# Expert lists padded to 128 rows instead of 256 in the mixture-of-experts stage of a four-stage kernel

## The chip, the core and the metric

The program runs on one core of a Trainium2 chip. The metric is device time in microseconds (us) for one execution; a comparison is made between medians of executions on the same chip. The core has five engines that run their own instruction streams and meet through semaphores: PE (TensorE, matrix products), DVE (VectorE), ACT (ScalarE), POOL (GpSimd) and SP (SyncE, which issues DMAs here). Times in a trace are us from the span's start unless marked ns.

## The reference, cut to what matters

Four layers run one after the other on an input of 2 x 2048 tokens of 128 features. The last one, cut from the reference, is the one that the change touches:

```python
x = hidden_states.reshape(T, D)                       # 4096 tokens of 128
logits = x @ gate_w + gate_b                          # 8 experts
probs = jax.nn.softmax(logits.astype(jnp.float32), axis=-1)
top_w, top_idx = jax.lax.top_k(probs, TOP_K)          # TOP_K = 2
top_w = top_w / jnp.sum(top_w, axis=-1, keepdims=True)
combine = jnp.zeros((T, NUM_EXPERTS), jnp.float32)
combine = combine.at[jnp.arange(T)[:, None], top_idx].set(top_w)
h = jax.nn.silu(jnp.einsum('td,edf->tef', x, w1)) * jnp.einsum('td,edf->tef', x, w3)   # f = 512
out_e = jnp.einsum('tef,efd->ted', h, w2)
out = jnp.einsum('ted,te->td', out_e, combine)
...
x = x + _layernorm(_L1_ffn_ref(_layernorm(x, axis=-1), ...), axis=-1)
```

The kernel computes only the two chosen experts of each token: 4096 tokens x 2 = 8192 pairs of a token and an expert.

## The kernel before, in words

The last stage is `phase_moe`. Its order is written out by hand in one list for each engine.

**Lists.** DVE finds the two experts of each token, counts the pairs of each expert and gives every pair a place: the pairs of an expert stand together, and each expert's list is padded to a whole number of tiles of ROWS = 256 rows. TILES = 39 tiles hold any split of 8192 pairs over 8 experts. `grid` and `tiles_of` count the tiles of an expert, `place` and `pos` the pair's place, `past` and `expert` the expert of each tile. The lists are turned by products with one-hot matrices (`hot_soon` for the first 16 columns of 128 rows, `hot_late` for the other COLS - 16 = 62) into `source`, the row that each place reads, and `to`, the row that it writes.

**Tile loop.** A tile of 256 rows goes through these steps:

- POOL issues two indirect DMAs that gather 128 rows each into `g` (`gather`, L2277), six tiles ahead (AHEAD = 6) into eight buffers.
- PE loads the tile's expert number from the list `expert` into a register (`expert_of`, L2133), and turns the rows by four products with the identity (`x_turn`, L2093); DVE copies them into `x16` (L2507).
- A tile has two units (u = 0, 1) of 256 hidden features. `up` makes a unit: for each of two blocks of 128 features, and for w1 (`R1`) and w3 (`R3`), one `product` of three matmuls in float16 parts (L2014 to L2016), with 256 columns. The weights' address depends on the expert's register (`of_expert`).
- ACT takes silu (L2231), DVE multiplies (L2523), ACT and DVE split the result into two float16 parts (L2217, L2514).
- `down` makes the second layer of a unit three units later (LAG = 3): twelve matmuls of 128 columns (L2126 to L2128), for two blocks of features and two halves r of 128 rows.
- ACT copies a finished tile to `y` (L2223), and POOL issues two indirect DMAs that scatter it to `moe_outs` (L2296).

PE's own order is

```python
for n in range(UNITS):
    i, u = divmod(n, 2)
    up(n, es[i])
    if u == 0 and i + 1 < TILES:
        es[i + 1] = expert_of(i + 1)
        x_turn(i + 1)
    if n >= LAG:
        down(n - LAG, es[(n - LAG) // 2])
```

and POOL's is, for each tile i: scatter tile i (two DMAs), then gather tile i + 6 (two DMAs).

**After the loop** SP reads `moe_outs` back, and DVE, ACT, POOL and PE add each token's two rows, normalise and add to `X`.

Of the kernel before, what the change touches and what calls it, by code (L numbers as in the profile page):

```python
# [8 lines left out]
ALU = mybir.AluOpType  # L9
# [3 lines left out]
P = 128  # L13
B = 2
T = 2048
# [9 lines left out]
E = 8  # L25
# [25 lines left out]
def build(nc, xT, vecs, att_w, cv_w, tern_w, hid_w, w3_w, ssm_w, dt_w, moe_w13, moe_w2, gate_w, consts, selectors, iota_c, outT,  # L51
# [3 lines left out]
    with ctx:  # L55
# [80 lines left out]
        if last_phase >= 4:  # L136
            phase_moe(nc, G)
        else:
            finish(nc, ctx, X, outT)
# [1717 lines left out]
def phase_moe(nc, G):  # L1857
# [6 lines left out]
    CHUNKS = GROUPS * TC  # L1864
    PAIRS = 2 * CHUNKS
    ROWS = 2 * P
    TILES = (PAIRS * P + E * (ROWS - 1)) // ROWS
    COLS = 2 * TILES
    UNITS = 2 * TILES
    PARTS = 8  # L1870
    PP = PAIRS // PARTS
    QUARTERS = 4
    QP = PAIRS // QUARTERS
    GRID = B * T // ROWS
    AHEAD, GR, HR, YR = 6, 8, 4, 4

    SOON, LATE = 16, COLS - 16
# [2 lines left out]
    with mem:  # L1880
        def sb(name, shape, dt=F32):
            return mem.enter_context(nc.sbuf_tensor(name, shape, dt))

        I32, U32 = mybir.dt.int32, mybir.dt.uint32
# [4 lines left out]
        lane_f = sb("lane_f4", [P, P])  # L1889
# [26 lines left out]
        so_far = sb("so_far4", [P, E, CHUNKS], F16)  # L1916
        grid = sb("grid4", [P, E, GRID])
        tiles_of = sb("tiles_of4", [P, E])
        tiles_to = sb("tiles_to4", [P, E])
# [6 lines left out]
        col_i = sb("col_i4", [P, PAIRS], I32)  # L1926
        col_h = sb("col_h4", [P, PAIRS], F16)
        low_h = sb("low_h4", [P, PAIRS], F16)
        past = sb("past4", [1, TILES, E])
        expert_f = sb("expert_f4", [1, TILES])  # L1930
        expert = sb("expert4", [1, TILES], I32)
        row_f = sb("row_f4", [P, COLS])
        empty = sb("empty4", [P, COLS])
        second = sb("second4", [P, COLS])
# [7 lines left out]
        x16 = sb("x16_4", [P, 2, 2, ROWS], F16)  # L1942
# [5 lines left out]
        w13_hi, w13_lo = G.moe_hi[:, 0:E, :], G.moe_lo[:, 0:E, :]  # L1948
        w2_hi, w2_lo = (w[:, E:, :].rearrange("p u m -> p (u m)").rearrange("p (e m) -> p e m", e=E)
                        for w in (G.moe_hi, G.moe_lo))  # L1950
# [18 lines left out]
        rank = XG[:, 1, 0:E * CHUNKS].rearrange("p (e c) -> p e c", e=E)  # L1969
# [24 lines left out]
        def _(sp):  # L1994
# [5 lines left out]
            for r in range(YR):  # L2000
                sp.wait_ge(S[f"scattered{r}"], 32 * len(range(r, TILES, YR)))
            by_pair = outs[0:P * PAIRS, :].rearrange("(p k c) d -> p k c d", k=2, c=CHUNKS)
# [9 lines left out]
        def _(pe):  # L2012
            def product(out, w_hi, w_lo, x_hi, x_lo, start, stop):
                nc.tensor.matmul(out, w_hi, x_hi, start=start, stop=False)  # L2014
                nc.tensor.matmul(out, w_hi, x_lo, start=False, stop=False)  # L2015
                return nc.tensor.matmul(out, w_lo, x_hi, start=False, stop=stop)  # L2016
# [54 lines left out]
            for q in range(PARTS):  # L2071
# [3 lines left out]
                for k in range(q * PP, (q + 1) * PP):  # L2075
                    last = nc.tensor.matmul(listed_soon, low_hot[:, k, :], hot_soon[:, k, 1:3, :].rearrange("p w c -> p (w c)"),
                                            start=k == 0, stop=k == PAIRS - 1)
            last.then_inc(S["listed"], 1)
            for q in range(QUARTERS):
                pe.wait_ge(S["hot_part"], q + 2)  # L2080
                pe.wait_ge(S["hot_pair"], q + 2)
                for k in range(q * QP, (q + 1) * QP):
                    last = nc.tensor.matmul(listed_late, low_hot[:, k, :], hot_late[:, k, 1:3, :].rearrange("p w c -> p (w c)"),  # L2083
                                            start=k == 0, stop=k == PAIRS - 1)
# [12 lines left out]
            def of_expert(w, e, m):  # L2097
                return w[:, bass.ds(e, 1), m].rearrange("p a m -> p (a m)")

            def up(n, e):
                i, u = divmod(n, 2)
                if u == 0:
                    pe.wait_ge(S["x_in"], i + 1)
                if n >= 2:
                    pe.wait_ge(S["hidden"], n - 1)
                for h in range(2):
                    for out, at in ((R1, 0), (R3, FFN)):
                        m = slice(at + (2 * u + h) * P, at + (2 * u + h + 1) * P)
                        last = product(out[:, u, h * ROWS:(h + 1) * ROWS], of_expert(w13_hi, e, m), of_expert(w13_lo, e, m),  # L2110
                                       x16[:, i % 2, 0, :], x16[:, i % 2, 1, :], True, True)
                last.then_inc(S["up"], 1)

            def down(n, e):
                i, u = divmod(n, 2)
                pe.wait_ge(S["hid_low"], n + 1)
                if u == 0 and i >= 2:
                    pe.wait_ge(S["y_out"], i - 1)
                for h in range(2):  # L2120
                    m = slice((2 * u + h) * P, (2 * u + h + 1) * P)
                    w_hi, w_lo = of_expert(w2_hi, e, m), of_expert(w2_lo, e, m)
                    for r in range(2):
                        out = Y[:, i % 2, r * P:(r + 1) * P]
                        at = slice(h * ROWS + r * P, h * ROWS + (r + 1) * P)
                        nc.tensor.matmul(out, hid_hi[:, n % HR, at], w_hi, start=u == 0 and h == 0 and r == 0, stop=False)  # L2126
                        nc.tensor.matmul(out, hid_hi[:, n % HR, at], w_lo, start=False, stop=False)  # L2127
                        last = nc.tensor.matmul(out, hid_lo[:, n % HR, at], w_hi,  # L2128
                                                start=False, stop=u == 1 and h == 1 and r == 1)
                last.then_inc(S["down"], 1)  # L2130

            def expert_of(i):
                return pe.value_load(expert[0:1, i:i + 1], min_val=0, max_val=E - 1)  # L2133

            pe.wait_ge(S["expert"], 1)
            es = {0: expert_of(0)}
            x_turn(0)
# [8 lines that stand above are left out]
            for n in range(UNITS - LAG, UNITS):  # L2146
                down(n, es[n // 2])

            for i in range(GROUPS):
# [3 lines left out]
                for j in range(TC):  # L2153
                    last = nc.tensor.matmul(R1[:, i % 2, j * P:(j + 1) * P], scaled[:, i % 2, j * P:(j + 1) * P], G.ident,
                                            start=True, stop=True)
# [159 lines left out]
        def _(dve):  # L2315
# [42 lines left out]
            def last_expert(v):  # L2358
# [18 lines left out]
                                           op0=ALU.mult, op1=ALU.add).then_inc(S["masked"], 1)  # L2377
# [21 lines left out]

            dve.wait_ge(S["counted"], 1)  # L2400
            steps = lane_f[:, 0:GRID].unsqueeze(1).to_broadcast([P, E, GRID])
            nc.vector.scalar_tensor_tensor(out=grid[:, :, :], in0=steps, scalar=float(ROWS),
                                           in1=counts.unsqueeze(2).to_broadcast([P, E, GRID]),
                                           op0=ALU.mult, op1=ALU.is_lt).then_inc(S["grid"], 1)
            dve.wait_ge(S["grid"], 1)
# [7 lines left out]
            dve.wait_ge(S["tiles_from"], 1)  # L2413
            dve.wait_ge(S["ranked"], 1)
            nc.vector.scalar_tensor_tensor(out=place[:, :, :], in0=tiles_from[:, :].unsqueeze(2).to_broadcast([P, E, CHUNKS]),
                                           scalar=float(ROWS), in1=rank, op0=ALU.mult, op1=ALU.add)\
              .then_inc(S["place"], 1)
            dve.wait_ge(S["place"], 1)
            nc.vector.tensor_tensor(placed[:, :, :, :], picks[:, :, :, :],
# [14 lines left out]
                                           op0=ALU.mult, op1=ALU.add).then_inc(S["low_h"], 1)  # L2434
# [39 lines left out]
            def targets(listed, c, n):  # L2474
                by_part = listed[:, 0:c.stop - c.start]
                nc.vector.scalar_tensor_tensor(out=empty[:, c], in0=by_part, scalar=0.0, in1=spare_f[:, c],
                                               op0=ALU.is_equal, op1=ALU.mult).then_inc(S["empty"], 1)
                nc.vector.scalar_tensor_tensor(out=row_f[:, c], in0=by_part, scalar=float(PAIRS), in1=row_f[:, c],
                                               op0=ALU.mult, op1=ALU.add).then_inc(S["row_f"], 1)
                dve.wait_ge(S["empty"], n + 1)  # L2480
                dve.wait_ge(S["row_f"], 2 * n + 2)
                nc.vector.scalar_tensor_tensor(out=to[:, c], in0=row_f[:, c], scalar=-float(PAIRS), in1=empty[:, c],
                                               op0=ALU.add, op1=ALU.add).then_inc(S["to"], 1)

            sources(listed_soon, slice(0, SOON), 0)
            for q in range(1, QUARTERS):
# [1 line left out]
                pair(hot_late, slice((q - 1) * QP, q * QP), LATE, q + 1)  # L2488
            pair(hot_late, slice((QUARTERS - 1) * QP, PAIRS), LATE, QUARTERS + 1)
            targets(listed_soon, slice(0, SOON), 0)  # L2490
            nc.vector.tensor_tensor(past[:, :, :], tiles_to[0:1, :].unsqueeze(1).to_broadcast([1, TILES, E]),
                                    lane_f[0:1, 0:TILES].unsqueeze(2).to_broadcast([1, TILES, E]), ALU.is_le)\
              .then_inc(S["past"], 1)
            dve.wait_ge(S["past"], 1)
            nc.vector.tensor_reduce(expert_f[:, :], past[:, :, :], AX.X, ALU.add).then_inc(S["expert_f"], 1)
# [22 lines left out]
            for n in range(UNITS):  # L2518
                i, u = divmod(n, 2)
                dve.wait_ge(S["silus"], n + 1)  # L2520
                if n >= HR:
                    dve.wait_ge(S["hid_low"], n - HR + 1)
                nc.vector.scalar_tensor_tensor(out=hid[:, n % HR, :], in0=R3[:, u, :], scalar=1.0 / WS,  # L2523
                                               in1=silu[:, u, :], op0=ALU.mult, op1=ALU.mult).then_inc(S["hidden"], 1)
# [105 lines left out]
```

## Time and profile before

| | |
|---|---|
| median of 3 executions | 1307.19 us (1306.41 to 1311.79) |
| the profiled execution, its own time | 1311.32 us |
| its span | 1309.6 us |
| mean granted clock of PE | 0.923 of 2.4 GHz |
| busy, share of the span | PE 82%, DVE 75%, ACT 56%, POOL 56% |
| tile loop: first register instruction of `up` to the last | 1065.2 to 1263.0 us |

The profiled execution is one of the program's executions with the hardware profiler on; its own time is 4.1 us above the median, and 1.7 us of it lie outside the span. A busy share is an average over the four stages, which have different limits; the tile loop is about 15% of the span, so it is read by windows of time and by single instructions. Matmuls are pipelined: a PE row's duration reaches past the start of the next, and the pace of PE is the distance between starts.

### The profile page before, as it was taken

How to read it: one execution, taken by the hardware profiler on the slowest of the kernel's cores; microseconds unless marked ns; L12 is line 12 of the kernel's file. 1: busy time of each engine (PE TensorE's matmuls, PEld its weight loads, DVE VectorE, ACT ScalarE, POOL GpSimd, SP SyncE). 2: the span in 40 equal slices, each digit the busy share in tenths (PEclk: the TensorE clock that was granted, in tenths of full speed). 3: DMA queues.
4: the chain of work that ended last, by engine and by line, in shares of the span. 5: the costliest groups of instructions: out<-in, count | busy, mean ns of one | idle time of the engine just before them, and what ended most of it. 6: DMA issues, size and time to landing. Idle time of an engine off the chain costs nothing. (4 is left out here: it accounts for less than half of the span.)

```text
span 1309.6 us, 16592 instructions
## 1 busy us (share of the span) xinstructions
PE 1072.4 (82%) x4914; PEld 542.1 (41%) x4914; DVE 987.7 (75%) x1333; ACT 733.9 (56%) x1163; POOL 737.6 (56%) x617
## 2 busy tenths in 40 slices
PE   6654679999999988989889898989788578887863
PEld 2211224444444432333333333434234468776753
DVE  6996776575755537999999999999992776655545
ACT  6774454555645445757667676757653345444444
POOL 0223342141422103899898989897984157777764
PEclk8885799999999998999999999999999579999996
DMA  6000000000000002323223222222220111111225
GB/s 226 1 1 0 0 1 1 1 2 1 0 0 0 1 0 90 105 72 103 75 92 93 84 89 88 65 73 72 66 65 0 65 28 50 53 49 51 49 46 192
DMA packets 32552, 67.07 MB, mean 51 GB/s; under 512 B 5760, under 2 KB 5952, under 8 KB 32256
## 3 DMA queue, kind: packets, MB, share of 16 engines
q1 hardware_dynamic: 27056, 55.16, 12.9%
q0 software_dynamic: 4992, 10.23, 2.9%
q8 instruction: 39, 0.64, 0.2%
q10 hardware_dynamic: 432, 0.76, 0.2%
q14 instruction: 33, 0.27, 0.1%
HBM read 56.57 MB, written 9.57 MB: 51 GB/s over the span
## 5 line engine op out<-in xcount | busy, mean ns | idle before, releaser
L1750 POOL TENSOR_TENSOR prod<-hs,csb 128x1024 f32<-128x1024 f32 x128 | 301.8, 2358 | 142.3 <-DVE hs L1797 141.6
L1797 DVE TENSOR_TENSOR_SCAN hs<-dA,carry,pD 128x512 f32<-128x512 f32 x256 | 313.7, 1267 | 5.2 <-DVE pD L1810 0.8
L1519 PE MATMUL pY<-prod,const 128*128 128x512 f32 x512 | 244.8, 601 | 1.8 <-POOL prod L1750 1.8
L1659 ACT ACTIVATE dA<-dt,negA 128x512 f32<-128x512 f32 x256 | 168.0, 713 | 17.3 <-POOL dt L1719 15.8
L1810 DVE TENSOR_TENSOR pD<-dtu,pD 128x1024 f32<-128x1024 f32 x128 | 155.6, 1216 | 9.7 <-PE pD L1533 9.6
L1519 PEld LDWEIGHTS pY<-prod,const 128*128 128x128 f32 x512 | 96.8, 192 | 117.7 <-issue 112.9
L2277 POOL DMA_INDIRECT g<-moe_rows,source x78 | 82.8, 1061 | 57.3 <-DVE source L2472 27.9
L2523 DVE SCALAR_TENSOR_TENSOR hid<-pR,silu 128x512 f32<-128x512 f32 x78 | 53.9, 691 | 68.0 <-ACT silu L2231 67.9
L1003 ACT ACTIVATE stage<-pR,vec 128x512 f32<-128x512 f32 x64 | 43.9, 687 | 100.2 <-PE pR L703 100.0
L2296 POOL DMA_INDIRECT moe_outs<-y,to x78 | 81.6, 1046 | 26.9 <-issue 23.2
L2231 ACT ACTIVATE silu<-pR 128x512 f32<-128x512 f32 x78 | 46.6, 597 | 75.7 <-PE pR L2016 75.7
L2014 PE MATMUL pR<-x,moe_hi 128*128 128x256 f16 x312 | 85.7, 275 | 2.4 <-DVE x L2507 2.4
L2015 PE MATMUL pR<-x,moe_hi 128*128 128x256 f16 x312 | 85.6, 274 | 0.0
L2016 PE MATMUL pR<-x,moe_lo 128*128 128x256 f16 x312 | 85.6, 274 | 0.0
L1448 PE MATMUL pQ<-xn,convw 128*128 128x512 f32 x112 | 61.5, 675 | 16.9 <-DVE xn L1780 16.9
L1053 POOL TENSOR_TENSOR z_lo<-z,z_hi 128x512 f16<-128x512 f32 x8 | 10.6, 1329 | 106.1 <-DVE z_hi L1140 106.1
L439 POOL TENSOR_TENSOR o<-o,rs 128x512 f32<-128x512 f32 x8 | 14.4, 1799 | 96.8 <-DVE o L559 96.8
L1533 PE MATMUL pD<-split,sel 96*128 96x512 bf16 x128 | 50.5, 395 | 19.0 <-DVE hs L1797 18.3
L1042 POOL TENSOR_TENSOR K_lo<-kstage,K_hi 128x512 f16<-128x512 f32 x24 | 28.8, 1204 | 53.7 <-DVE K_hi L1115 53.7
L2126 PE MATMUL pY<-moe_hi,hid_hi 128*128 x312 | 56.7, 220 | 0.8 <-DVE hid_lo L2514 0.8
L2128 PE MATMUL pY<-moe_hi,hid_lo 128*128 x312 | 56.6, 220 | 0.0
L2127 PE MATMUL pY<-moe_lo,hid_hi 128*128 x312 | 56.6, 220 | 0.0
(423 smaller groups left out, 2573.9 us busy)
## 6 DMA issues: line engine op xcount, KB each, us to landing
csb<-ssm_c SPq DMA_DIRECT2D x128, 256.0 KB, 3.1
raw<-moe_w SPq DMA_DIRECT2D x12, 512.0 KB, 4.9
room<-moe_outs SPq DMA_DIRECT2D x8, 512.0 KB, 7.9
hidw<-hid_w SPq DMA_DIRECT2D x1, 2048.0 KB, 10.0
moe_rows<-xt SPq DMA_DIRECT2D x8, 256.0 KB, 2.0
outT<-X SPq DMA_DIRECT2D x8, 256.0 KB, 2.0
X<-xT SPq DMA_DIRECT2D x3, 512.0 KB, 4.1
g<-moe_rows,source POOLq DMA_INDIRECT x78, 2.8
```

The source lines that it names most:

```text
L1448: last = nc.tensor.matmul(Q[c][:], convw[:, c, k, :], xn[b][:, k:k + N], start=k == 0, stop=k == TAPS - 1)
L1519: last = nc.tensor.matmul(YB[c][:], G.ident, prod[:, slot(b, n), c, :], start=n == 0, stop=n == DST - 1)
L1659: last = nc.scalar.activation(dA[:, slot(b, n), c, :], dt[:, b, c, :], ACT.Exp, scale=negA[:, c, n:n + 1])
L1750: nc.gpsimd.tensor_tensor(prod[:, slot(b, n), :, :], hs[:, slot(b, n), :, :], csb[:, slot(b, n), :, :].to_broadcast([P, CB, N]), ALU.mult)\
L1797: last = nc.vector.tensor_tensor_scan(hs[:, slot(b, n), c, :], dA[:, slot(b, n), c, :], dBu(n, c), carry[:, b, n, c:c + 1], ALU.mult, ALU.add)
L1810: nc.vector.tensor_tensor(DD[:, (n % 2) * CB:(n % 2) * CB + CB, :], dtu[:, b, :, :], bcastB(n).unsqueeze(1).to_broadcast([P, CB, N]), ALU. ...
L2014: nc.tensor.matmul(out, w_hi, x_hi, start=start, stop=False)
L2015: nc.tensor.matmul(out, w_hi, x_lo, start=False, stop=False)
L2016: return nc.tensor.matmul(out, w_lo, x_hi, start=False, stop=stop)
L2126: nc.tensor.matmul(out, hid_hi[:, n % HR, at], w_hi, start=u == 0 and h == 0 and r == 0, stop=False)
L2277: nc.gpsimd.indirect_dma_start(g[:, i % GR, r, :], None, rows, bass.IndirectOffsetOnAxis(ap=source[:, 2 * i + r:2 * i + r + 1], axis=0))\
L2296: nc.gpsimd.indirect_dma_start(outs, bass.IndirectOffsetOnAxis(ap=to[:, 2 * i + r:2 * i + r + 1], axis=0), y[:, i % YR, r, :], None).then_ ...
```

## The change

The unit of padding becomes 128 rows. An expert's list is padded to a multiple of 128, TILES becomes 36, and a tile still has 256 rows, but its two halves r = 0, 1 may belong to two experts. So PE loads two expert numbers for each tile, and every product of `up` is made for each half apart, with 128 columns and the half's own weights. `down` takes its weights inside the loop over halves.

```diff
-    TILES = (PAIRS * P + E * (ROWS - 1)) // ROWS
+    TILES = ((PAIRS * P + E * (P - 1)) // P + 1) // 2
...
-    GRID = B * T // ROWS
+    GRID = B * T // P
...
-        past = sb("past4", [1, TILES, E])
-        expert_f = sb("expert_f4", [1, TILES])
-        expert = sb("expert4", [1, TILES], I32)
+        past = sb("past4", [1, COLS, E])
+        expert_f = sb("expert_f4", [1, COLS])
+        expert = sb("expert4", [1, COLS], I32)
...
                         m = slice(at + (2 * u + h) * P, at + (2 * u + h + 1) * P)
-                        last = product(out[:, u, h * ROWS:(h + 1) * ROWS], of_expert(w13_hi, e, m), of_expert(w13_lo, e, m),
-                                       x16[:, i % 2, 0, :], x16[:, i % 2, 1, :], True, True)
+                        for r in range(2):
+                            s = slice(r * P, (r + 1) * P)
+                            last = product(out[:, u, h * ROWS + r * P:h * ROWS + (r + 1) * P], of_expert(w13_hi, e[r], m),
+                                           of_expert(w13_lo, e[r], m), x16[:, i % 2, 0, s], x16[:, i % 2, 1, s], True, True)
...
-                    w_hi, w_lo = of_expert(w2_hi, e, m), of_expert(w2_lo, e, m)
                     for r in range(2):
+                        w_hi, w_lo = of_expert(w2_hi, e[r], m), of_expert(w2_lo, e[r], m)
...
-                return pe.value_load(expert[0:1, i:i + 1], min_val=0, max_val=E - 1)
+                return [pe.value_load(expert[0:1, c:c + 1], min_val=0, max_val=E - 1) for c in (2 * i, 2 * i + 1)]
...
-            nc.vector.scalar_tensor_tensor(out=grid[:, :, :], in0=steps, scalar=float(ROWS),
+            nc.vector.scalar_tensor_tensor(out=grid[:, :, :], in0=steps, scalar=float(P),
...
-                                           scalar=float(ROWS), in1=rank, op0=ALU.mult, op1=ALU.add)\
+                                           scalar=float(P), in1=rank, op0=ALU.mult, op1=ALU.add)\
...
-            nc.vector.tensor_tensor(past[:, :, :], tiles_to[0:1, :].unsqueeze(1).to_broadcast([1, TILES, E]),
-                                    lane_f[0:1, 0:TILES].unsqueeze(2).to_broadcast([1, TILES, E]), ALU.is_le)\
+            nc.vector.tensor_tensor(past[:, :, :], tiles_to[0:1, :].unsqueeze(1).to_broadcast([1, COLS, E]),
+                                    lane_f[0:1, 0:COLS].unsqueeze(2).to_broadcast([1, COLS, E]), ALU.is_le)\
```

COLS = 2 x TILES goes from 78 to 72, so `hot_late` from 62 columns to 56 and `past` from 312 numbers to 576; GRID goes from 16 to 32.

```order
L2014 ISA
L2014 MATMUL pR3_4<-x16_4,moe_hi 128x256
L2015 MATMUL pR3_4<-x16_4,moe_hi 128x256
L2016 REGISTER_ALU
L2016 MATMUL pR3_4<-x16_4,moe_lo 128x256
```

And now, for the same block of features:

```order
L2014 ISA
L2014 MATMUL pR3_4<-x16_4,moe_hi 128x128
L2015 MATMUL pR3_4<-x16_4,moe_hi 128x128
L2016 REGISTER_ALU
L2016 MATMUL pR3_4<-x16_4,moe_lo 128x128
L2014 ISA
L2014 MATMUL pR3_4<-x16_4,moe_hi 128x128
L2015 MATMUL pR3_4<-x16_4,moe_hi 128x128
L2016 REGISTER_ALU
L2016 MATMUL pR3_4<-x16_4,moe_lo 128x128
```

One pair of register instructions stood ahead of 768 columns, and now stands ahead of 384.

The second place is PE at the end of the first unit of a tile, where it loads the next tile's expert (expert4) and turns its rows (g4). Before:

```order
L2016 REGISTER_ALU
L2016 MATMUL pR3_4<-x16_4,moe_lo 128x256
L2133 TENSOR_LOAD expert4
L2133 ISA x2
L2093 MATMUL pX4<-ident16_4,g4 128x128 x4
```

And now:

```order
L2016 REGISTER_ALU
L2016 MATMUL pR3_4<-x16_4,moe_lo 128x128
L2135 TENSOR_LOAD expert4
L2135 ISA x2
L2135 TENSOR_LOAD expert4
L2135 ISA x2
L2093 MATMUL pX4<-ident16_4,g4 128x128 x4
```

A second load with its two followers stands between `up` and `x_turn`.

The third place is one block of features of `down` on PE (hid_hi4 and hid_lo4 are the parts of the hidden layer). Before:

```order
L2126 ISA
L2126 MATMUL pY4<-moe_hi,hid_hi4 128x128
L2127 REGISTER_ALU
L2127 MATMUL pY4<-moe_lo,hid_hi4 128x128
L2128 MATMUL pY4<-moe_hi,hid_lo4 128x128
L2126 MATMUL pY4<-moe_hi,hid_hi4 128x128
L2127 MATMUL pY4<-moe_lo,hid_hi4 128x128
L2128 MATMUL pY4<-moe_hi,hid_lo4 128x128
```

And now:

```order
L2128 ISA
L2128 MATMUL pY4<-moe_hi,hid_hi4 128x128
L2129 REGISTER_ALU
L2129 MATMUL pY4<-moe_lo,hid_hi4 128x128
L2130 MATMUL pY4<-moe_hi,hid_lo4 128x128
L2128 ISA
L2128 MATMUL pY4<-moe_hi,hid_hi4 128x128
L2129 REGISTER_ALU
L2129 MATMUL pY4<-moe_lo,hid_hi4 128x128
L2130 MATMUL pY4<-moe_hi,hid_lo4 128x128
```

The matmuls are the same six; the second half has a pair of register instructions of its own. Over the whole program PE had 312 pairs in `up` and 156 in `down` and now has 576 and 288; it had 39 loads of an expert number and now has 72. The waits of PE keep their places: one ahead of `x_turn` (L2090), one ahead of the first unit of a tile (L2106), one ahead of the first `down` of a tile (L2119, now L2121).

## Rows read from the trace of the kernel before

**Rows 1.** The page's part 4, the chain that ended last, by line.

```profile
POOL moe_outs L2296 4%; POOL g L2277 3%; DMA g<-moe_rows,source 1%; PE pX L2034 1%; DVE room L2451 1%; DMA room<-moe_outs 1%; DVE room L2438 0%; DVE hid L2538 0%; ACT convw L2245 0%; PE pR L2014 0%; PE pR L2016 0%; PE pR L2015 0%; PE pY L2083 0%; DVE room L2444 0%; PE pX L2026 0%
```

**Rows 2.** Groups of instructions from 980 us on: POOL's indirect DMAs (busy, mean ns | idle before).

```profile
L2277 POOL DMA_INDIRECT g<-moe_rows,source x78 | 82.8, 1061 | 57.3 <-DVE source L2472 27.9 <-issue 21.0 <-PE pR L2016 7.1
L2296 POOL DMA_INDIRECT moe_outs<-y,to x78 | 81.6, 1046 | 26.9 <-issue 23.2 <-ACT y L2223 3.7
```

**Rows 3.** Timeline of POOL: start, duration, engine, line, what [idle before].

```profile
1234.06 1.05 POOL L2296 DMA_INDIRECT moe_outs<-y,to  x1 [0.30 <-issue]
...
1239.52 1.05 POOL L2296 DMA_INDIRECT moe_outs<-y,to  x1 [0.30 <-issue]
```

**Rows 4.** Timeline of PE: down, up and the wait ahead of the next x_turn.

```profile
1155.70 0.22 PE L2126 MATMUL pY<-moe_hi,hid_hi 128*128 x1
...
1156.37 0.27 PE L2014 MATMUL pR<-x,moe_hi 128*128 128x256 f16 x1
...
1157.57 0.27 PE L2016 MATMUL pR<-x,moe_lo 128*128 128x256 f16 x1
1158.99 0.40 PE L2093 MATMUL pX<-ident,g 128*128 128x128 f16 x4 [1.15 <-DMA g<-moe_rows,source]
```

**Rows 5.** PE's expert loads from 1073 to 1095 us: ns min/median/max, first and last start.

```profile
L2133 PEldq TENSOR_LOAD <-expert x6: 297/302/308, 1073.3 to 1094.1; - x6
L2133 PEldq FUSED_REGOPS  x6: 151/151/151, 1073.7 to 1094.5; - x6
L2133 PEldq SEQ_ASSERT  x6: 18/18/18, 1073.9 to 1094.7; - x6
```

**Rows 6.** Lines L2014, L2016 and L2106 over the whole span, columns as in rows 5.

```profile
L2014 PEldq FUSED_REGOPS  x312: 46/46/51, 1065.2 to 1262.9; - x156
L2016 PEldq ALU_OP  x312: 32/32/38, 1065.3 to 1263.0; - x156
L2016 PE MATMUL pR<-x,moe_lo x312: 272/273/421, 1065.5 to 1264.4; 128*128 128x256 f16 x156
L2106 PEldq EVENT_SEMAPHORE  x38: 51/51/51, 1068.2 to 1260.5; - x38
```

**Rows 7.** Lines L2014 and L2126 from 1070.6 to 1072.0 us, and from 1074.0 to 1076.0 us.

```profile
L2014 PEldq FUSED_REGOPS  x4: 46/46/46, 1070.7 to 1071.4; - x4
...
L2126 PEldq FUSED_REGOPS  x2: 46/53/60, 1071.7 to 1071.9; - x2
...
L2126 PEldq FUSED_REGOPS  x4: 46/46/60, 1074.1 to 1075.9; - x4
...
L2014 PEldq FUSED_REGOPS  x4: 46/46/46, 1074.6 to 1075.4; - x4
```

**Rows 8.** Timeline of DVE while the lists are made.

```profile
1034.82 0.29 DVE L2402 SCALAR_TENSOR_TENSOR grid<-lane_f,pR 128x128 f32<-128x128 f32 x1 [0.29 <-PE pR L2067]
...
1050.40 1.18 DVE L2438 TENSOR_TENSOR room<-lane_h,col_h 128x992 f16<-128x992 f16 x1
...
1060.51 0.47 DVE L2491 TENSOR_TENSOR past<-tiles_to,lane_f 1x312 f32<-1x312 f32 x1
...
1062.70 0.22 DVE L2461 TENSOR_SCALAR second<-pY 128x62 f32<-128x62 f32 x1 [1.01 <-PE pY L2083]
```

**Rows 9.** Windows: length, busy of PE, PEld, DVE, ACT, POOL, granted clock, DMA share, GB/s.

```profile
1097.00:1204.00 107.00, 88.05 (x1059) 77.97 (x1060) 65.06 (x101) 52.12 (x101) 82.32 (x82) 1.00 0.18 51
1206.70:1210.10 3.40, 1.25 (x19) 0.96 (x17) 1.48 (x3) 1.11 (x2) 2.79 (x3) 1.00 0.21 65
1210.10:1213.50 3.40, 3.40 (x24) 2.65 (x22) 0.93 (x2) 0.79 (x2) 2.49 (x4) 0.50 0.19 33
```

**Rows 10.** Timeline of PE at the lower clock, an `up` and the `down` behind it.

```profile
1210.29 0.42 PE L2014 MATMUL pR<-x,moe_hi 128*128 128x256 f16 x1
...
1212.85 0.31 PE L2126 MATMUL pY<-moe_hi,hid_hi 128*128 x1
1212.95 0.31 PE L2127 MATMUL pY<-moe_lo,hid_hi 128*128 x1
```

## The prediction

> **What bounds the kernel now.** The change lies in the tile loop of the last stage, so I looked first at what sets the pace there. The chain that ended last [rows 1] holds three lines of this loop and names POOL's two, the scatter and the gather, ahead of PE's products; the other pieces are of other stages or of the ends of this one. The groups [rows 2] say why: 156 indirect DMAs, 1.05 us each, and after nearly each 0.3 us that the view calls issue. Busy 82.8 + 81.6 and idle 57.3 + 26.9, less the 27.9 us that POOL waited for the first list, make 220.7 us, 1.41 us for a call. A tile's four calls need 4 x (1.05 + 0.30) = 5.4 us, and in the timeline of POOL [rows 3] the first scatters of two tiles stand 5.46 us apart (1234.06 to 1239.52), with the 0.30 ahead of each: POOL is full.
>
> PE waits for it. In its timeline [rows 4] twelve matmuls of `down` take 1155.70 to 1156.37, 0.056 us each, each with weights of its own; the twelve of `up` with 256 columns go at 0.109 us (eleven steps, 1156.37 to 1157.57); and then the next `x_turn` waits 1.15 us for a gather. The array's work for a tile is 24 x 0.109 + 24 x 0.056 + 4 x 0.056 = 4.2 us, which is the pace early in the loop, while gathers were still ahead: expert loads recur every 4.16 us (1073.3 to 1094.1 in five tiles, [rows 5]). Over the whole loop, from the first register instruction of `up` at 1065.2 to the last at 1263.0 [rows 6], 39 tiles take 197.8 us, 5.1 us each.
>
> There is a third clock in this loop, which no busy time shows: PE's sequencer. Each product costs it two register instructions, FUSED_REGOPS of 46 ns and ALU_OP of 32 ns [rows 6]. Their durations are not their price. The price is read from starts where nothing held the sequencer [rows 7]: four FUSED_REGOPS of an `up` from 1070.7 to 1071.4 and two of the `down` behind it at 1071.7 and 1071.9 are six starts, five pairs in 1.2 us, 0.24 us a pair. The next such stretch goes from 1074.1 through the `up` at 1074.6 to 1075.4 to the `down` that ends at 1075.9: eight starts, seven pairs in 1.8 us, 0.257 us. A pair of `down` is followed by six matmuls and one of `up` by three, and both cost about a quarter of a microsecond: it is the register instructions that cost, not the matmuls. I take 0.245.
>
> An expert load takes the sequencer from 1073.3 (TENSOR_LOAD, 0.30 us) over FUSED_REGOPS (0.15) to SEQ_ASSERT at 1073.9 [rows 5], with what follows it about 0.65 us. A wait that is already met lasts 51 ns [rows 6]; a register instruction takes 0.24 / 2 = 0.12 us for durations near 0.04, some 0.08 more than it shows, so I estimate a wait at 0.11 to 0.13 and take 0.11. The sequencer's work for a tile before is then 12 x 0.245 + 0.65 + 3 x 0.11 = 3.9 us. So for each tile now: POOL 5.4, the array 4.2, the sequencer 3.9. It hides behind both.
>
> **The change, part by part.** *POOL* issues 144 calls in place of 156. At 1.41 us that is 17 us off the engine that bounds the loop; for a tile its work stays at 5.4 to 5.7 us.
>
> *The array* streams the same columns for a tile: 48 matmuls of 128 columns in `up`, for 24 of 256. If 128 columns take what they take in `down`, 0.056 [rows 4], the tile needs 76 x 0.056 = 4.26 us, as before. The upper bound is the 0.109 of a 256-column product, if new weights set the pace: 48 x 0.109 + 28 x 0.056 = 6.8 us. I take 0.056, since `down` has a weight load for each matmul just as the new `up` will. The Trainium skill, "TensorE: Matmul & The Clock Gate", section on the back-to-back issue gap, speaks against that: it puts a sustained stream of weight loads and 128-column matmuls at about 81 ns each. By it the tile would be 76 x 0.081 = 6.2 us; the trace of `down`, at 56 ns, does not agree.
>
> *The sequencer* gets 8 pairs for each `up` in place of 4, 4 for each `down` in place of 2, and two expert loads. A tile costs 24 x 0.245 + 2 x 0.65 + 3 x 0.11 = 7.5 us. That is more than POOL's 5.4 and the array's 4.3, so the sequencer becomes the bound of the loop. With both of its price's ends: if a pair cost only its durations, 46 + 32 = 78 ns, the tile would be 3.5 us and nothing would be lost; with 0.257 it is 7.8.
>
> Summed from the loop's first pair to the last pair of the last `up`, as the 197.8 us were: 864 pairs less the 12 of the last three `down`s are 852 x 0.245 = 208.7; 70 expert loads (all but the first tile's) x 0.65 = 45.5; 34 + 35 + 34 waits x 0.11 = 11.3. Together 265.5 us, and **+67.7** against 197.8. With 0.24 and 0.257 for a pair the sum is 261.3 or 275.8, +63 to +78.
>
> What is queued behind the longer stream does not add to it, as far as I can see. `up` waits for the silu and product of the unit two before, `down` for the split of the unit three before; early in the loop they kept up with a unit in 2.1 us (half of 4.16, [rows 5]), and a unit will take 3.7. The gathers, now late by 1.15 us [rows 4], will be early: POOL needs 5.4 to 5.7 us for a tile of 7.5. So that wait goes, and ACT, DVE and POOL all wait for PE.
>
> *After the loop's last `up`* the array stood 1.4 us behind its sequencer (last matmul 1264.4, last ALU_OP 1263.0, [rows 6]); paced by the sequencer it will stand about 0.3 behind: **-1.1**.
>
> *The lists.* The late one-hot matrices have 56 columns for 62. Eight DVE operations at 1.18 us, such as the one at 1050.40 [rows 8], lie on the way to the first tile; 6/62 of each is 0.11, **-0.9** together. `grid` doubles to 256 elements: the two operations that make and sum it, 0.29 us for the first [rows 8], cost at most as much again each, **+0.4** taken. `past` and its sum, 0.47 us [rows 8] for 312 numbers, grow to at most 0.87 each, 0.8 us that falls into the 1.01 us that DVE then waits for PE [rows 8]; without that cover it would be +0.8. The second load of the first tile's experts runs while DVE still works on the late list. Net -0.5.
>
> **Sum:** 67.7 - 1.1 - 0.5 = +66 us. The profiled execution, 1311.3 us (1.7 of it around the span), would become 1377; the median shown is 4.1 lower, so 1307.2 + 66 = **1373 us**, 5% slower.
>
> **The rivals.** *POOL stays the bound (faster).* Then the register instructions hide in the array's time, 12 calls x 1.41 = 17 us go, and with the lists 0.5: 1290 us. This is what the smaller count of tiles gives by itself. It decides where the new sequencer sum equals 197.8 + 1.6 us: (199.4 - 45.5 - 11.3) / 852 = 0.167 us for a pair. Below that the kernel is faster; the rows show 0.24 at the least. For it speaks only that these starts were read beside an array that was itself busy, so that part of the 0.24 could be a queue that was full; against it that three and six matmuls to a pair give the same. Chance 0.04.
>
> *Weights set the array's pace and the sequencer doesn't bind.* At the bound of 6.8 us a tile the loop takes 36 x 6.8 = 245 us, +47, less 1.6 for the lists and the end: 1352 us. Against it speaks the 0.056 of `down`, and that the sequencer asks for 7.5 anyway. Chance 0.03. By the 81 ns of the Trainium skill's page, "TensorE: Matmul & The Clock Gate", section on the back-to-back issue gap, it would be 36 x 6.2 = 222, +23, 1330 us.
>
> *The array falls to its lower clock.* Before, the granted clock was 1.00 through 107 us of the loop with PE busy for 88, and 0.50 (1.2 of 2.4 GHz) from 1210.1 to 1213.5, after 3.4 us in which PE was busy for 1.25 [rows 9]. There a 256-column matmul took (1212.85 - 1210.29) / 12 = 0.213 us and a 128-column one 0.10 to 0.107 [rows 10]. The array's share will be 4.26 / 7.5 = 57% of the time, with 1.3 us of expert loads in one piece, so it may fall now and then. All the way at 0.107 a tile needs 76 x 0.107 = 8.1 us, more than the sequencer's 7.5: 293 us, +95, less 1.6: 1400 us. At the lower clock PE would be busy throughout, as it was in [rows 9], after which the clock rose again; so I expect at most stretches of it, with few us lost since the two lie close. Chance 0.08 that it costs over 15 us.
>
> *No change.* Within 0.5% (6.5 us, about what a measurement of this kernel can tell from none) needs a pair at 0.16 to 0.175 us, or the weights' pace near 5.6 us a tile. Chance 0.02, taken with the first rival's.
>
> **How the numbers follow.** Forecast 0.83, lower clock 0.08, weights' pace 0.03, POOL 0.04, no change 0.02. The forecast alone lies between 1307.2 + 63 - 1.6 = 1369 and 1307.2 + 78 - 1.6 = 1384; a slightly smaller load price and the profile's rounding to tenths widen it to 1360 below, and part of the lower clock to 1396 above. POOL and the weights' pace stay outside. Faster by over 0.5%: 0.04; within: 0.02; slower: 0.94.
>
> **What the profile will show.** Right: the loop lasts some 265 us; expert loads come in twos every 7.3 to 7.6 us; `x_turn` waits for no gather; PE is idle between products, with starts of `up`'s 128-column matmuls in threes every 0.24 us; POOL's idle time grows and is ended by ACT's `y` and by PE. Wrong: starts of `up` evenly 0.056 apart with pauses ahead of `x_turn` (POOL), evenly 0.08 or more at full clock (weights), or a granted clock of 0.50 through much of the loop.

## The result and the profile after

The changed kernel takes 1381.95 us (median of four runs, 1378.11 to 1384.39), the kernel before 1306.8 us beside it (1304.47 to 1311.79). The ratio on record is 1.0554, with a 95% interval of 1.0523 to 1.0585, and the ratio of these two medians, 1.0575, lies inside it. Of the executions told of below, one of the ten of experiment 4 took 5880.68 us at a granted clock of 0.173, where the others took 1307.72 to 1315.14, and the ratio of that experiment leaves it out. The profiled execution took 1383.79 us, its span is 1382.0, 72.4 more than the 1309.6 of before.

The page's part 4, the chain that ended last, by line, after (it answers to [rows 1]):

```profile
PE pR L2014 5%; PE pR L2016 3%; PE pR L2015 2%; PE pY L2129 2%; PE pY L2128 2%; PE pY L2130 1%; PE pX L2093 1%; DVE room L2453 1%; DMA room<-moe_outs 1%; DVE room L2440 0%; DVE room L2446 0%; POOL sq L2312 0%; DVE hid L2540 0%; DMA moe_rows<-xt 0%; PE pX L2034 0%
```

POOL's scatter and gather have left the list; PE's products stand in their place. Lines L2014 and L2016 over the whole span, after (operation, count: ns min/median/max, first and last start; it answers to [rows 6]):

```profile
L2014 PEldq FUSED_REGOPS  x576: 46/46/56, 1065.4 to 1337.5; - x192
...
L2016 PEldq ALU_OP  x576: 32/32/38, 1065.5 to 1337.7; - x192
...
L2016 PE MATMUL pR<-x,moe_lo x576: 216/219/314, 1065.6 to 1337.8; 128*128 128x128 f16 x192
```

From the first register instruction of `up` to the last, the loop lasts 1337.7 - 1065.4 = 272.3 us, where [rows 6] gave 197.8. The last matmul stands 0.1 us behind the last ALU_OP, where it stood 1.4 behind: the array no longer has a queue. The expert loads between 1100 and 1300 us, after (it answers to [rows 5]):

```profile
L2135 PEldq TENSOR_LOAD <-expert x52: 294/297/311, 1102.7 to 1296.6; - x52
L2135 PEldq FUSED_REGOPS  x52: 151/151/151, 1103.1 to 1297.0; - x52
L2135 PEldq SEQ_ASSERT  x52: 18/18/18, 1103.3 to 1297.2; - x52
```

52 loads are 26 tiles, so from first to last start lie 25 tiles and one load (0.65): (1296.6 - 1102.7 - 0.65) / 25 = 7.73 us a tile. The timeline of PE shows how such a tile looks (it answers to [rows 4]):

```profile
1202.12 0.23 PE L2014 MATMUL pR<-x,moe_hi 128*128 128x128 f16 x1
1202.18 0.22 PE L2015 MATMUL pR<-x,moe_hi 128*128 128x128 f16 x1
1202.24 0.22 PE L2016 MATMUL pR<-x,moe_lo 128*128 128x128 f16 x1
1202.36 0.23 PE L2014 MATMUL pR<-x,moe_hi 128*128 128x128 f16 x1
...
1202.59 0.23 PE L2014 MATMUL pR<-x,moe_hi 128*128 128x128 f16 x1
1202.66 0.22 PE L2015 MATMUL pR<-x,moe_hi 128*128 128x128 f16 x1
1202.77 0.22 PE L2016 MATMUL pR<-x,moe_lo 128*128 128x128 f16 x1
1202.89 0.23 PE L2014 MATMUL pR<-x,moe_hi 128*128 128x128 f16 x1
...
1204.71 0.38 PE L2093 MATMUL pX<-ident,g 128*128 128x128 f16 x4 [1.25 <-issue]
```

Starts come in threes, 0.06 apart, and the threes 0.24 apart: from the last start of a product to the first of the next it is 0.12 us, of which 0.06 is a matmul's own pace and 0.06 is a wait for the next addresses. One three is stretched: 0.11 between L2015 and L2016, and the next product 0.30 behind (1202.59 to 1202.89). Ahead of `x_turn` there is a pause of 1.25 us as there was one of 1.15 before, but its cause is another. It is put down to issue, and to no gather; the two expert loads stand in it (TENSOR_LOAD at 1203.3 and 1203.9, the last SEQ_ASSERT at 1204.5). Waits from 1064 to 1340 us, after (waiter, waited for: us in total, times, longest):

```profile
DVE hid L2525 <- ACT silu L2233: 148.1, 72, 3.5
ACT silu L2233 <- PE pR L2016: 138.2, 72, 7.3
POOL moe_outs L2298 <- ACT y L2225: 100.6, 34, 6.1
PEld pX L2093 <- issue: 49.6, 36, 2.7
...
PE pR L2014 <- DVE x L2509: 0.9, 1, 0.9
```

ACT waits for PE, and DVE and POOL wait for ACT. The last line is the only wait of PE's matmuls for another engine in the whole loop. POOL's groups, after (it answers to [rows 2]):

```profile
L2279 POOL DMA_INDIRECT g<-moe_rows,source x72 | 72.7, 1010 | 58.2 <-DVE source L2474 25.3 <-issue 20.7 <-PE pR L2016 12.2
L2298 POOL DMA_INDIRECT moe_outs<-y,to x72 | 71.0, 987 | 116.1 <-ACT y L2225 103.6 <-issue 12.5
```

POOL makes 144 calls of 1.0 us for 156 of 1.05, and it now waits 103.6 us for `y` ahead of its scatters, where it waited 3.7. Windows after, columns as in [rows 9]:

```profile
1069.00:1200.00 131.00, 109.65 (x1295) 84.47 (x1293) 56.75 (x87) 44.09 (x84) 65.43 (x67) 1.00 0.12 35
1200.00:1328.00 128.00, 107.13 (x1255) 82.05 (x1253) 53.70 (x83) 43.68 (x84) 62.61 (x64) 1.00 0.13 35
1328.00:1340.00 12.00, 11.44 (x136) 10.11 (x136) 5.78 (x9) 5.10 (x10) 3.88 (x4) 0.86 0.05 18
```

The granted clock stays at full speed through 259 of the loop's us; it was lower only in the first and the last few. And PE's busy share, 84%, hides that the array pauses after every product, since a matmul row of 0.22 us reaches over the 0.12 us to the next start: the share is much as it was in [rows 9], 82%, with another engine as the bound.

DVE while the lists are made, after (it answers to [rows 8]):

```profile
1035.73 0.42 DVE L2404 SCALAR_TENSOR_TENSOR grid<-lane_f,pR 128x256 f32<-128x256 f32 x1 [0.29 <-PE pR L2067]
...
1051.58 1.08 DVE L2440 TENSOR_TENSOR room<-lane_h,col_h 128x896 f16<-128x896 f16 x1
...
1060.92 0.74 DVE L2493 TENSOR_TENSOR past<-tiles_to,lane_f 1x576 f32<-1x576 f32 x1
...
1062.59 0.20 DVE L2463 TENSOR_SCALAR second<-pY 128x56 f32<-128x56 f32 x1
```

The wait of 1.01 us ahead of `second` has gone into `past` and its sum, as the prediction put it.

### The profile page after: what moved, and what is told of

The parts are those of the page before. It is cut to its first block and busy times, and to the rows that moved or that the text cites. A ratio compares the mean times of both kernels' runs of the same rounds, so it can differ in the third digit from the quotient of the medians.

```text
span 1382.0 us, 18812 instructions
## 1 busy us (share of the span) xinstructions
PE 1134.0 (82%) x5622; PEld 567.8 (41%) x5622; DVE 978.6 (71%) x1318; ACT 727.3 (53%) x1148; POOL 717.0 (52%) x605
## 5 line engine op out<-in xcount | busy, mean ns | idle before, releaser
L2525 DVE SCALAR_TENSOR_TENSOR hid<-pR,silu 128x512 f32<-128x512 f32 x72 | 49.8, 692 | 148.1 <-ACT silu L2233 148.1
L2014 PE MATMUL pR<-x,moe_hi 128*128 128x128 f16 x576 | 131.5, 229 | 0.9 <-DVE x L2509 0.9
L2298 POOL DMA_INDIRECT moe_outs<-y,to x72 | 71.0, 987 | 116.1 <-ACT y L2225 103.6
L2015 PE MATMUL pR<-x,moe_hi 128*128 128x128 f16 x576 | 126.9, 221 | 0.0
L2016 PE MATMUL pR<-x,moe_lo 128*128 128x128 f16 x576 | 126.5, 220 | 0.0
L2233 ACT ACTIVATE silu<-pR 128x512 f32<-128x512 f32 x72 | 43.0, 597 | 138.2 <-PE pR L2016 138.2
L2279 POOL DMA_INDIRECT g<-moe_rows,source x72 | 72.7, 1010 | 58.2 <-DVE source L2474 25.3
L2014 PEld LDWEIGHTS pR<-x,moe_hi 128*128 x576 | 55.7, 97 | 31.2 <-issue 1.2
L2128 PE MATMUL pY<-moe_hi,hid_hi 128*128 x288 | 63.5, 227 | 0.7
L2130 PE MATMUL pY<-moe_hi,hid_lo 128*128 x288 | 62.7, 219 | 0.0
L2129 PE MATMUL pY<-moe_lo,hid_hi 128*128 x288 | 62.5, 218 | 0.2
```

What stands on the lines that cost most here:

```text
L2130: last = nc.tensor.matmul(out, hid_lo[:, n % HR, at], w_hi, start=False, stop=u == 1 and h == 1 and r == 1)
L2279: nc.gpsimd.indirect_dma_start(g[:, i % GR, r, :], None, rows, bass.IndirectOffsetOnAxis(ap=source[:, 2 * i + r:2 * i + r + 1], axis=0))\
```

## Experiments

The theory is that PE's sequencer, with its register instructions and expert loads, sets the pace of the loop. Against it stand the rivals that 128 columns for each set of weights, or the array itself, set it, and that the price goes by something other than the number of register instructions. "The loop" is, below, the time from the first to the last start of the matmuls of L2016: 198.9 us before (1065.5 to 1264.4, [rows 6]) and 272.2 after.

**1. No addresses to work out.** The products take their weights from fixed places; the loads of the expert numbers stay. The weights are then those of the wrong experts.

```diff
-                return w[:, bass.ds(e, 1), m].rearrange("p a m -> p (a m)")
+                return w[:, e, m]
...
-                return [pe.value_load(expert[0:1, c:c + 1], min_val=0, max_val=E - 1) for c in (2 * i, 2 * i + 1)]
+                for c in (2 * i, 2 * i + 1):
+                    pe.value_load(expert[0:1, c:c + 1], min_val=0, max_val=E - 1)
+                return [0, 1]
```

> The kernel after, but the weights of every product stand at an address known when the program is built (the first half of a tile takes expert 0, the second expert 1), so that no register instruction is left in up and down; the two expert numbers of a tile are still read, and tiles, columns and products are those of after. The output is not the reference's, since the wrong experts' weights are used. Theory (PE's sequencer is the bound, at about 0.255 us for each pair of register instructions): the loop falls back to GpSimd's pace, 36 of the 39 tiles of before, 197.8 x 36/39 = 182.6 us, so 1307 - 15 - 1 = about 1291 us (1284 to 1298). Rival (128 columns for each load of weights set TensorE's own pace, 6.8 us a tile): it stays at 1352 us or above.

Measured: 1294.81 us, 0.9876 of the kernel before in the same session (0.9827 to 0.9926). Its chain by line, and L2016:

```profile
POOL moe_outs L2300 4%; POOL g L2281 3%; DMA g<-moe_rows,source 1%; DVE room L2455 1%; POOL g L2275 0%; DVE room L2442 0%; DVE room L2448 0%; PE pR L2158 0%; DVE hid L2542 0%; ACT convw L2249 0%; DMA room<-moe_outs 0%; PE pR L2014 0%; PE pR L2016 0%; PE pR L2015 0%; POOL sq L2314 0%
```

```profile
L2016 PE MATMUL pR<-x,moe_lo x576: 219/219/314, 1064.5 to 1249.1; 128*128 128x128 f16 x192
```

The same 76 matmuls a tile, the same columns and the same weight loads run in a loop of 184.6 us, POOL leads the chain again, and `x_turn` waits for gathers again (25.4 us in 25 waits, in the trace of this run). The loss hangs on the register instructions; the rival that weights set the pace has fallen.

**2. One register instruction for a product.** The two addresses are worked out next to each other, ahead of the product's first matmul, and the program then has one FUSED_REGOPS where it had FUSED_REGOPS and ALU_OP. Nothing of the computation changes.

```diff
+            def addressed(stationary, *weights):
+                for w in weights:
+                    nc.tensor.lower_ap(w, for_matmul_weights=stationary)
+                return weights
...
-                            last = product(out[...], of_expert(w13_hi, e[r], m), of_expert(w13_lo, e[r], m), ...)
+                            w_hi, w_lo = addressed(True, of_expert(w13_hi, e[r], m), of_expert(w13_lo, e[r], m))
+                            last = product(out[...], w_hi, w_lo, ...)
...
-                        w_hi, w_lo = of_expert(w2_hi, e[r], m), of_expert(w2_lo, e[r], m)
+                        w_hi, w_lo = addressed(False, of_expert(w2_hi, e[r], m), of_expert(w2_lo, e[r], m))
```

> The kernel after, but with both addresses of a product (high and low part of the weights) worked out side by side ahead of its first product, so that one register instruction does it where two did. Theory in the form that an instruction on PE's sequencer costs its own duration (46 ns) and about 80 ns more, whatever it works out: 24 x 0.13 + 2 x 0.65 + 3 x 0.11 = 4.8 us a tile, below GpSimd's 5.4, so as with fixed addresses about 1291 us (1284 to 1300). Rival 1 (the price goes by the number of operations worked out, which stays): no change against after, 1375 to 1385. Rival 2 (the weights set TensorE's pace): no change, 1382.

Measured: 1292.55 us, 0.9867 of before (0.981 to 0.9924). Its addresses over the whole span, and from 1152 to 1153.5 us, then its expert loads from 1100 to 1240 us:

```profile
L2102 PEldq FUSED_REGOPS  x864: 55/55/74, 1065.4 to 1252.6; - x173
...
L2102 PEldq FUSED_REGOPS  x10: 55/55/60, 1152.0 to 1153.3; - x10
```

```profile
L2141 PEldq TENSOR_LOAD <-expert x54: 296/305/399, 1101.6 to 1237.0; - x54
```

A gather of POOL, and the one four calls later:

```profile
1150.10 0.99 POOL L2285 DMA_INDIRECT g<-moe_rows,source  x1 [0.30 <-issue]
...
1155.28 0.99 POOL L2285 DMA_INDIRECT g<-moe_rows,source  x1 [0.30 <-issue]
```

One instruction that does the work of both lasts 55 ns, and ten of them start within 1.3 us, 0.14 us each, where a pair took 0.24 and more. A tile takes (1237.0 - 1101.6 - 0.65) / 26 = 5.18 us. The price goes by the number of instructions, then; that it goes by what they work out, and that the weights set the pace, are both off by more than 80 us. Nor does it go by where the second instruction stands: in the trace after, the ALU_OP in the middle of an `up` product starts 0.124 us behind its FUSED_REGOPS, with two matmuls between, and the next FUSED_REGOPS 0.113 us behind the ALU_OP, with one (medians). With 24 x 0.14 + 1.3 + 0.33 = 5.0 us the sequencer is close to POOL's 5.2 (1150.10 to 1155.28), nearer than the 4.8 that was expected, and in its chain by line PE's products lead, while POOL's scatter and gather are not among the lines:

```profile
PE pR L2014 3%; PE pR L2016 3%; PE pR L2015 3%; PE pY L2134 1%; PE pY L2136 1%; PE pY L2135 1%; PE pX L2093 1%; PE pX L2034 1%; DVE room L2459 1%; DMA room<-moe_outs 1%; DVE room L2446 0%; DVE room L2452 0%; POOL sq L2318 0%; DVE hid L2546 0%; PE pR L2162 0%
```

POOL and PE now take about as long for a tile, and the time is that of experiment 1, with no pairs at all. This version beats the kernel before as well, by 1.3% (0.8 to 1.9): it keeps the 36 tiles and pays little for the second expert.

**3. One expert load for a tile.** The second half takes its expert number from the first's. Its weights are then the wrong ones.

```diff
-                return [pe.value_load(expert[0:1, c:c + 1], min_val=0, max_val=E - 1) for c in (2 * i, 2 * i + 1)]
+                e = pe.value_load(expert[0:1, 2 * i:2 * i + 1], min_val=0, max_val=E - 1)
+                return [e, E - 1 - e]
```

> The kernel after, but with one expert number read for each tile and the second half's taken from it (expert 7 - e); all 24 pairs of register instructions of a tile stay. The second half of a tile gets the wrong expert's weights. Theory: where the sequencer is the bound, 36 reads of 0.645 us fall away, -23 us: about 1359 us (1354 to 1364). Rival (TensorE's array or its weights set the pace, the sequencer runs beside it): the reads are hidden, no change against after, 1378 to 1384.

Measured: 1358.43 us, 1.0383 of before (1.0336 to 1.0431), 23.5 below the changed kernel's median (22 by the two ratios, (1.0554 - 1.0383) x 1307). Its expert loads from 1100 to 1300 us and, over the whole span, an instruction that the edit adds and the matmuls of L2016:

```profile
L2135 PEldq TENSOR_LOAD <-expert x28: 298/302/364, 1100.5 to 1294.3; - x28
...
L2014 PEldq MOVE  x36: 29/29/35, 1058.8 to 1306.8; - x36
...
L2016 PE MATMUL pR<-x,moe_lo x576: 216/219/314, 1058.8 to 1311.7; 128*128 128x128 f16 x192
```

A tile takes (1294.3 - 1100.5) / 27 = 7.18 us, 0.55 less than 7.73. The load saved is 0.65; the MOVE gives back about 0.1 (an estimate, from the 0.029 that it lasts and the 0.08 that stood behind the other register instructions). So the second load is paid in full, which it would not be if the sequencer had room. (Part of the 23.5 is no saving of the loop: between the two traces the loop is 272.2 - 252.9 = 19.3 us shorter, and begins 6.8 us earlier, because the stages ahead of it ended earlier. That the time came so close to the 1359 us expected is in part luck.)

**4. The 128 columns alone.** The kernel before, with `up` in products of 128 columns and both halves by one address.

```diff
-                        last = product(out[:, u, h * ROWS:(h + 1) * ROWS], of_expert(w13_hi, e, m), of_expert(w13_lo, e, m),
-                                       x16[:, i % 2, 0, :], x16[:, i % 2, 1, :], True, True)
+                        w_hi, w_lo = of_expert(w13_hi, e, m), of_expert(w13_lo, e, m)
+                        for r in range(2):
+                            s = slice(r * P, (r + 1) * P)
+                            last = product(out[:, u, h * ROWS + r * P:h * ROWS + (r + 1) * P], w_hi, w_lo,
+                                           x16[:, i % 2, 0, s], x16[:, i % 2, 1, s], True, True)
```

> The kernel before (39 tiles, one expert each, 12 pairs of register instructions a tile), but with up in products of 128 columns, both halves by the same address. Theory (the columns are not the cause; the sequencer has nothing more to do but issue): no change against before, 1303 to 1311. Rival (new weights for every 128 columns set TensorE's pace at 6.8 us a tile): 39 x 6.8 = 265 us where 197.8 was, about 1374 us.

Measured: 1312.57 us, 1.0017 of before (0.9994 to 1.004): no change, though just above the range expected (the kernel before took 1309.42 us beside it). Timeline of PE, first matmuls of three products in a row:

```profile
1149.84 0.22 PE L2014 MATMUL pR<-x,moe_hi 128*128 128x128 f16 x1
...
1150.01 0.22 PE L2014 MATMUL pR<-x,moe_hi 128*128 128x128 f16 x1
...
1150.17 0.22 PE L2014 MATMUL pR<-x,moe_hi 128*128 128x128 f16 x1
```

0.165 us for three matmuls of 128 columns, each with a load of weights, is 0.055 each: the price that the prediction took from `down`. The Trainium skill, "TensorE: Matmul & The Clock Gate", section on the back-to-back issue gap, has 81 ns for such a stream; this trace does not agree.

**5. The 36 tiles alone.** The lists of after, with the matrix code of before, which takes the first half's expert for the whole tile; the second half may get wrong weights. In `up` and `down` the edit undoes the change's own; beside that:

```diff
...
-                return [pe.value_load(expert[0:1, c:c + 1], min_val=0, max_val=E - 1) for c in (2 * i, 2 * i + 1)]
+                return pe.value_load(expert[0:1, 2 * i:2 * i + 1], min_val=0, max_val=E - 1)
```

> The lists and the 36 tiles of after with the matrix code of before: one expert for each tile (that of its first half), up in products of 256 columns, 12 pairs of register instructions and one read a tile. The second half of a tile can get the wrong expert's weights. It shows what the smaller number of tiles is worth where PE's sequencer has room. Theory (GpSimd sets the pace): as with fixed addresses, 1288 to 1296 us. Rival (what the smaller number of tiles saves in the loop is taken back by the lists or by the way from the loop to the end): no change against before, 1304 to 1310.

Measured: 1295.21 us, 0.9889 of before (0.9828 to 0.995). Fewer tiles are worth some 14 us; the loss of the whole change is that of the matrix code with its second expert load, about 87 us (1381.95 - 1295.21).

**6. One register instruction in the kernel before.** `addressed`, as in experiment 2, for its 12 products a tile.

```diff
-                        last = product(out[:, u, h * ROWS:(h + 1) * ROWS], of_expert(w13_hi, e, m), of_expert(w13_lo, e, m),
+                        w_hi, w_lo = addressed(True, of_expert(w13_hi, e, m), of_expert(w13_lo, e, m))
+                        last = product(out[:, u, h * ROWS:(h + 1) * ROWS], w_hi, w_lo,
                                        x16[:, i % 2, 0, :], x16[:, i % 2, 1, :], True, True)
...
-                    w_hi, w_lo = of_expert(w2_hi, e, m), of_expert(w2_lo, e, m)
+                    w_hi, w_lo = addressed(False, of_expert(w2_hi, e, m), of_expert(w2_lo, e, m))
```

> The kernel before, with both addresses of a product worked out in one register instruction (12 a tile where there were 24). Theory (before, the sequencer's work lies beside GpSimd's and sets nothing): no change, 1303 to 1311 us, and what the one instruction gives the changed kernel is not a gain that before could have had too. Rival (the sequencer's time is part of the path before already, ahead of each wait of GpSimd for the matrix engine): 39 x 12 x 0.12 = 56 us or a part of it, 1300 us or less.

Measured: 1310.32 us, 1.001 of before (0.9981 to 1.0038): no change. 39 x 12 = 468 instructions fewer in the loop, and nothing of it is seen in the time, because POOL sets the pace there. The same edit is worth 89 us once 24 products a tile have made the sequencer the bound.

## Why the prediction was right

**The bound that moves.** This is the step on which the forecast stood, and it held: PE's sequencer takes over from POOL. Experiments 1 and 2 show it from one side (without the pairs POOL's calls lead the chain again, and with half of their instructions the loop falls to POOL's pace), 3 from the other (a load less on it is time less). That six matmuls to a pair cost what three do was the argument ahead; experiment 1, with all matmuls and no pairs, is the proof.

**The size.** The forecast was 6 to 9 us short: +66 against 72.4 in the profiled executions and 75 in the medians. The term that was mis-sized is the price of a pair. With 70 loads at 0.65 and 103 waits at 0.11 as forecast, (272.3 - 45.5 - 11.3) / 852 = 0.253 us is left for a pair, for the 0.245 taken; 852 of them are then 215.5 us for 208.7, which is the whole of +74.5 against +67.7 in the loop. The two stretches of [rows 7] gave 0.24 and 0.257, and the lower one came out of ends rounded to tenths: to the nanosecond, the trace before has the first stretch from 1070.659 to 1071.907, 0.250 for a pair, and the second from 1074.100 to 1075.887, 0.255. Together that is 0.253, what the loop then took.

The timeline after shows how such a mean comes about: most steps are 0.24, but some, like the one at 1202.59, are stretched. Over the trace after, the ALU_OP starts 0.125 us behind its FUSED_REGOPS at the median, and 0.15 us or more in 190 of the 864 pairs. That isn't scatter. Where no expert load lies between, two such pairs stand four products apart in 138 of 155 cases, and eight or twelve in the others. What stretches about every fourth product isn't settled; no run here took it apart.

**After the loop.** The array's lag went from 1.4 to 0.1, -1.3 for the -1.1 forecast. From the last ALU_OP to the end of the span it is 44.3 us now (1382.0 - 1337.7) and was 46.6; the other 1.0 was not forecast and may be the executions' own scatter. So may be the 0.9 us by which `grid` starts later (1035.73 for 1034.82); with it the parts add up to the 72.4 of the spans.

**The lists.** From the start of `grid` to the first register instruction of `up`: 1065.4 - 1035.73 = 29.7 now, 1065.2 - 1034.82 = 30.4 before, -0.7 for the -0.5 forecast. The one-hot operations took 1.08 for 1.18, `grid` 0.42 for 0.29, and the longer `past` (0.74 for 0.47) fell into the wait.

**The rivals.** POOL staying the bound, 1290 us, is what experiments 1, 2 and 5 measure (1292.6 to 1295.2, 14 to 17 us below the kernel before beside them; 17 was forecast): its mechanism was sized well, and it fails in the changed kernel because a pair costs 0.253. The 0.167 that the prediction names is where the loop would be as long as before; for POOL to be the bound again, a pair would have to cost (197.8 - 17 - 45.5 - 11.3) / 852 = 0.146 or less. In experiment 2 a product costs 0.14, just below that point, and the rival's time comes true, with PE and POOL about level. The weights' pace fell with experiments 1 and 4. The lower clock did not come: 1.00 from 1069 to 1328 us, all but some us at either end of the loop.

## What to carry to other kernels

An address that comes from a register cost time on PE's sequencer here, which no busy share shows: before a loop's tiles are given more addresses or more loaded numbers, add up these instructions, from start to start and not by their durations, and compare the sum with the bound of the loop. Where the sum comes out above, work the addresses of one product out side by side, so that they fuse into one instruction: the price went mostly by the instruction, not by what it computes. And take the price of such an instruction as a mean over a long stretch, not from a few starts in a quiet one whose ends are rounded to tenths.

## What the hardware showed that was not expected

FUSED_REGOPS for both addresses lasts 55 ns, for one 46: the second address costs 9 ns when it shares an instruction and about 0.11 us when it has its own (0.253 for a pair, 0.14 for one). The indirect DMAs of the changed kernel are a little shorter, a mean of 1010 and 987 ns for 1061 and 1046; why isn't shown. In the changed kernel about every fourth product is stretched, and it isn't shown why. And the clock held at 1.00 with pauses of 0.06 us after every product and of 1.25 us in a tile, where it had fallen to 0.50 once before, behind a stretch in which PE was busy for 1.25 of 3.4 us [rows 9].
